# The experts' down projection with the tokens as the stationary side, in a fused attention and mixture-of-experts block

## The reference

```python
def _experts(x_flat, Wg, Wu, Wd):
    g = jax.nn.silu(jnp.einsum('nc,eci->nei', x_flat, Wg))
    u = jnp.einsum('nc,eci->nei', x_flat, Wu)
    return jnp.einsum('nei,eic->nec', g * u, Wd)

def _moe(x, Wgate, expert_bias, Wg, Wu, Wd, sWg, sWu, sWd):
    shared = jnp.mean(_experts(xf, sWg, sWu, sWd), axis=1)
    ...
    routed = jnp.einsum('ne,nec->nc', comb, _experts(xf, Wg, Wu, Wd))
    return (shared + routed).reshape(b, t, c)

xn = _layernorm(x, axis=-1)
x = x + _L0_attn_ref(xn, ...) + _L0_ffn_ref(xn, ...)
```

## Time and profile before

| | |
|---|---|
| median of 3 runs | 1395.76 us (1391.84 to 1400.21) |
| the profiled execution, first to last instruction | 1398.2 us |
| mean granted TensorE clock | 0.960 of full |
| busy share | PE 94%, PEld 66%, DVE 78%, ACT 60%, POOL 51% |
| HBM traffic over the span | 107 GB/s |

### The profile page before, as it was taken

One profiled execution on the slowest core, in us unless ns is written; L12 is line 12 of the kernel. 1 busy time (PEld: TensorE's weight loads), 2 busy tenths in 40 slices (PEclk: granted clock), 3 DMA queues, 4 the chain that ended last, 5 costly groups with the idle time before them and its releaser, 6 DMA issues.

```text
span 1398.2 us, 40108 instructions
## 1 busy us (share of the span) xinstructions
PE 1309.8 (94%) x16484; PEld 923.2 (66%) x16484; DVE 1085.4 (78%) x2298; ACT 844.3 (60%) x1329; POOL 710.1 (51%) x800
## 2 busy tenths in 40 slices
PE   4589999999999999999999999999999999999996
PEld 3456666666766676676766767676666766666654
DVE  7767687977979787887879788887878888787623
ACT  1046566666666666666666666666666666666662
POOL 4434454565455566545555665545556554545112
PEclk8679899999999999999999999999999999999998
DMA  6655455435455544555555445545544454555000
GB/s 192 109 120 125 113 135 128 119 67 124 110 132 136 124 114 85 119 115 124 136 136 125 107 94 112 127 117 135 135 114 113 81 125 113 136 128 125 13 2 16
DMA packets 139993, 156.43 MB, mean 112 GB/s; under 512 B 32896, under 2 KB 126756, under 8 KB 133668
## 3 DMA queue, kind: packets, MB, share of 16 engines
q1 hardware_dynamic: 139812, 153.87, 46.9%
HBM read 83.10 MB, written 67.11 MB: 107 GB/s over the span
## 4 chain that ended last, share of the span: by engine, by line
PE 77%; DVE 12%; POOL 6%; issue 2%; ACT 1%; SPq 1%; DMA 0%; POOLq 0%; DVEq 0%
PE ps L226 24%; PE psm L226 18%; PE pse L226 13%; PE psv L226 13%; DVE R L771 6%; PE ps L353 3%; POOL x2lo L1382 1%; POOL tc_ L1336 1%; PE ps L344 1%; PE ps L419 1%; DVE pB L726 1%; PE ps L361 1%; PE ps L413 1%; POOL kt_ L1345 1%; DVE rt L854 1%
## 5 line engine op out<-in xcount | busy, mean ns | idle before, releaser
L771 DVE TRANSPOSE_TENSOR_REDUCE R<-psm 128x32 f32<-128x1024 f32 x384 | 478.6, 1246 | 163.4 <-PE psm L226 160.5
L1146 ACT ACTIVATE PT<-pse 128x1024 f32<-128x1024 f32 x384 | 393.8, 1025 | 278.3 <-PE pse L226 278.1
L1328 POOL TENSOR_TENSOR ts_<-ts_,pA 128x512 f32<-128x512 f32 x32 | 37.1, 1158 | 374.3 <-DVE pA L717 374.3
L226 PE MATMUL pse<-qsB,ks 128*128 128x512 f32 (+1 forms) x768 | 215.4, 417 | 2.3 <-ACT pse L1150 2.3
L226 PE MATMUL psm<-qsB,ksm 128*128 128x256 f32 (+1 forms) x640 | 139.6, 333 | 20.6 <-DVE R L771 13.6
L1387 POOL TENSOR_TENSOR hT<-th,cbs 128x512 f32<-128x512 f32 x64 | 82.0, 1282 | 132.3 <-ACT cbs L1200 132.2
L1150 ACT ACTIVATE pse<-maskb 128x512 f32<-128x512 bf16 x256 | 143.4, 593 | 4.1
L1160 ACT ACTIVATE OT<-psv 128x512 f32<-128x512 f32 x128 | 76.8, 600 | 93.5 <-PE psv L226 91.6
L226 PEld LDWEIGHTS pse<-qsB,ks 128*128 128x128 f32 (+1 forms) x768 | 108.1, 194 | 32.2 <-ACT pse L1150 13.0
L226 PEld LDWEIGHTS psm<-qsB,ksm 128*128 128x128 f32 x640 | 96.3, 195 | 47.9 <-DVE R L771 30.7
L226 PE MATMUL psv<-PT,vA 128*9 128x128 f32 x3072 | 100.5, 279 | 4.7 <-issue 4.7
(11 more groups left out here) (196 smaller groups left out, 2683.0 us busy)
## 6 DMA issues: line engine op xcount, KB each, us to landing
scrB<-pB SPq DMA_DIRECT2D x64, 768.0 KB, 5.0
qsB<-scrB SPq DMA_DIRECT2D x128, 384.0 KB
scrA<-pA SPq DMA_DIRECT2D x128, 96.0 KB, 2.3
qsA<-scrA SPq DMA_DIRECT2D x128, 64.0 KB
ksA<-scrA SPq DMA_DIRECT2D x128, 64.0 KB
xs<-in_x SPq DMA_DIRECT2D x16, 256.0 KB, 2.9
qsA<-scrA SPq DMA_DIRECT2D x128, 32.0 KB
ksA<-scrA SPq DMA_DIRECT2D x128, 32.0 KB
```

The source lines that it names most:

```text
L226: return e.matmul(o, l, r, start=start, stop=stop, skip_group_check=True)
L771: e.tensor_reduce(red, MX[:].rearrange("p i (c q) -> p (i c) q", q=32), AX.X, ALU.max, apply_transpose=True).then_inc(s_mr, 1)
L1146: e.activation(PT[g % 4], EX[:], ACT.Exp, scale=(8.0 ** -0.5, 0.125)[br]).then_inc(s_pt, 1)
L1328: e.tensor_tensor(rA[:], fA[:], pA[:, 0], ALU.subtract).then_inc(s_ra, 1)
```

## The change

- PE's `moe_d` makes, for each of the five slices, four products instead of one: the stationary side is a block of 128 tokens of `hT`, the moving side `wds` of that slice with its 128 columns. The output has the tokens in the partitions, in four column blocks of the same bank, which is the layout that the transposes gave.
- `moe_t` on PE, `moe_d` on ACT and the tile `dT` go. `moe_out` reads the bank `wd` itself; it is the one that frees it.
- On DVE `moe_out` stands at k = 2 ahead of `stats` and `prep_a0` instead of behind them.
- The shared slice is used with all 128 partitions. POOL sets partitions 64 to 127 of slice 4 of `hT` and of `wds` to zero at the start, between `stats2(0)` and `stats(1)`, and PE's first down projection waits for that.
- `store` waits for the release of `wd`, and `moe_sq` on ACT, which writes `th[0]`, waits for POOL's last `moe_h` of the pair before instead of for the release of `mt`.

```diff
-        sq, dT = th[0], th[1]
+        sq = th[0]
...
                 if fs[0] == 4:
                     wd[0] = claim(w, now, 2, "wd", p)
                     w.wait_ge(s_wb, WD)
+                    w.wait_ge(s_pad, 2)
                 bk, s = wd[0]
                 for f in fs:
-                    M = 128 if f < 4 else 64
                     if f < 4:
                         w.wait_ge(s_h, 4 * p + f + 1)
                     else:
                         released(w, "g", 4, p)
-                    t = mm(bk[:], wds[0:M, f, :], hT[0:M, f, :], f == 4, f == 3)
+                    for i in range(4):
+                        t = mm(bk[:, 128 * i:128 * i + 128], hT[:, f, 128 * i:128 * i + 128], wds[:, f, :], f == 4 and i == 0, f == 3)
...
-            def moe_t(p):
-                bk, f = claim(w, now, 0, "mt", p)
-                released(w, "wd", p)
-                for i in range(4):
-                    t = e.transpose(bk[:, 128 * i:128 * i + 128], dT[:, 128 * i:128 * i + 128], ident[:])
-                t.then_inc(f, 1)
...
                     if k == 3:
-                        if even and done:
-                            moe_t(p - 1)
                         if before:
                             tail_out(c - 1)
...
             def moe_out(p):
-                bk, f = arrived(w, "mt", p)
+                bk, f = arrived(w, "wd", p)
...
                     if k == 2:
+                        if even and done:
+                            moe_out(p - 1)
                         if soon3:
                             stats(n2 + 1)
                         if soon:
                             prep_a0(n2)
                         if odd and moe:
                             moe_hg(p, 4)
-                        if even and done:
-                            moe_out(p - 1)
...
             def moe_sq(p, a):
                 w.wait_ge(s_y, 2 * p + 2)
-                if p >= 1:
-                    released(w, "mt", p - 1)
+                w.wait_ge(s_h, 4 * p)
...
-            def moe_d(p):
-                bk, f = arrived(w, "wd", p)
-                e.activation(dT[:], bk[:], ACT.Copy).then_inc(f, 1)
...
                     if k == 2:
-                        if even and done:
-                            moe_d(p - 1)
                         if odd and moe:
                             moe_c(p)
...
             stats2(0)
+            w.wait_ge(s_pw2, 1)
+            e.memset(hT[64:128, 4, :], 0.0).then_inc(s_pad, 1)
+            w.wait_ge(s_pad, 1)
+            e.memset(wds[64:128, 4, :], 0.0).then_inc(s_pad, 1)
+            w.wait_ge(s_pad, 2)
             stats(1)
...
             def store(p):
-                released(w, "mt", p)
+                released(w, "wd", p)
```

More of the change, by code:

```diff
@@ L169, in build @@
             sem(n) for n in ("s_half", "s_k1", "s_ksi", "s_wa", "s_wn", "s_wb", "s_sa", "s_sb"))
-        s_bv = sem("s_bv")
+        s_bv, s_pad = sem("s_bv"), sem("s_pad")
         s_v, s_g = sem("s_v"), sem("s_g")
```

## The result

| | before | changed |
|---|---|---|
| median, same chip | 1397.65 us (1391.84 to 1400.21, 4 runs) | 1415.43 us (1406.87 to 1419.13, 4 runs) |
| changed / before | | 1.0115, 95% interval 1.0066 to 1.0165 |
| span of the profiled execution | 1398.2 us | 1405.1 us |

The changed kernel is slower by 1.15% (by the two medians alone it would be 1.27%). Ratios, here and in the table of the experiments, are worked out from the faster group of executions alone, while medians and ranges take in all of them, so the two need not agree. The forecast was 1406.5 us and its range ended at 1413: the sign was right, the size was too small. The profiled execution of the changed kernel is the fastest of its four runs, so its span understates the loss.

What follows compares the result with a forecast made beforehand. The prediction took PE to bound the kernel (77% of the chain). Thirteen pairs (+12.3), two pairs without `prep_qk` (-0.4) and the end (-1.2) gave +10.7 us on the median 1395.8: 1406.5 us, range 1397 to 1413.

Steps and rivals of the forecast that it cites:

- products, a pair: PE's down projection: 40 passes of 128 columns instead of 10 of 512 cost +0.18 us a pair.
- change from 64 to 128 rows, padding: PE's down projection: padding costs no columns and the row change merely moves to the step's start; costed at zero.
- transposes, a pair: On PE in even blocks, removing the four transposes of the product is worth -0.40 us a pair.
- wait of `prep_qk` for DVE, a pair: PE's `prep_qk` waits for its bank until DVE's `moe_out`, behind the k = 2 reduction, frees it: +1.17 us.
- together, 13 pairs: Products, wait and transposes summed where `prep_qk` follows the down projection: +0.95 us each, +12.3 in all.
- the pairs without `prep_qk`: At c = 30 and 32 the bank goes to `tail_out`, without a wait: -0.22 us each, -0.4 in all.
- start, memsets: Two POOL memsets between `stats2(0)` and `stats(1)`: cost 0, at worst 0.2 us, or 2.3 once without cover.
- end: After the last product DVE starts 0.04 us later, without ACT and transposes between: -1.2 us once.
- A: Rival: the stall at `prep_qk` is covered, so the kernel is not slower, 1391.3 us; chance 0.15.
- B: Rival: stall covered and earlier `moe_out` shortens the k = 3 reduction's turn on DVE, 1382 us; chance 0.03.
- C: Rival: PE's weight loads show, a pass every 0.192 us instead of 0.112, 1458 us; chance 0.03.
- I put the change on the median: Baseline step: +10.7 us added to the median of the runs, 1395.8, instead of the profiled span, 1398.2.

Runs made afterwards that it cites:

- e4: Changed kernel, but ACT copies the down projection's bank to `dT` at k = 2 and frees it, `moe_out` adds from `dT`; 1395.63 us, ratio 0.9976.
- e5: e4 with the old products of 512 columns and transposes left out, so its output is not the reference's; 1391.44 us, ratio 0.9979.
- e7: Changed kernel with 64 rows again for the shared slice instead of the padded 128; 1408.04 us, ratio 1.0079.
- e6: Kernel before, but DVE instead of ACT copies the bank to `dT`, behind the k = 2 reduction; 1413.42 us, ratio 1.0122.
- e1: The changed kernel, unaltered, timed again beside the kernel before; 1412.9 us over 11 runs, ratio 1.0078.
- e12: The same kernel as e11, run again for a readable trace; 1409.64 us, ratio 1.0119.
- e2: Changed kernel with `moe_out` on DVE ahead of the k = 2 reduction instead of behind it; 1395.09 us, ratio 0.9977.
- e10: Kernel before with the first shared gate product moved from ahead of the k = 9 scores to behind them; 1391.44 us, ratio 0.9945.
- e11: Changed kernel with the first shared gate product moved behind the k = 9 scores; 1414.5 us, ratio 1.0088.
- e9: e2 with the first shared gate product moved from ahead of the k = 9 scores to behind them; 1386.45 us, ratio 0.9917.
- e3: Changed kernel with `moe_out` on DVE behind `stats` instead of ahead of it; 1461.07 us, ratio 1.0434.
- e8: Changed kernel with an unneeded DVE memset of 485 ns ahead of `moe_out`; 1437.46 us, ratio 1.0303.

## Why the prediction missed

**The terms were right.** Against the steps of the forecast, in its order:

| step of the forecast | forecast | measured | where |
|---|---|---|---|
| products, a pair | +0.18 | +0.17 | e4 less e5; 16 passes on the chain 1.79 us, four before 1.72 |
| change from 64 to 128 rows, padding | 0 | 0.01 at most | e7 |
| transposes, a pair | -0.40 | -0.38 | e5 |
| wait of `prep_qk` for DVE, a pair | +1.17 | +1.14 to 1.17 | changed, e6 |
| together, 13 pairs | +0.95 each | +0.93 to 0.96 in 12 (once 1.02), 0.72 or 0.73 in one | changed, e1, e12 |
| the pairs without `prep_qk` | -0.22 each | -0.21 to -0.22 at c = 30; c = 32 has no reductions to compare | changed, e1, e12 |
| start, memsets | 0 | 0: 200 ns the smaller; DVE's next step at 10.10, before 10.11 | changed |
| end | DVE 0.04 behind the product | 1401.61 against 1396.94 + 4.63 = 1401.57 | changed |

The wait was foreseen with its engine, its line and its number. Only its look was off: I expected 1.1 to 1.4 us of idle each in the view, and it shows 0.9 at the matmul and 1.1 at the weight load, since the idle is counted from the end of the last matmul's record, and before, `prep_qk` began while that record still ran (1.14 less 0.89, so 0.25 us).

**The rivals.** A (covered) falls: e2 and e4 show what a kernel without the wait does, -0.21, and the changed one has +0.93. B falls with it. C (weight loads show) falls: 16 passes of 128 columns, each with its load of 192 ns, take 1.79 us, 0.112 each. This bears also on the rule of the Trainium skill that was weighed ("TensorE: Matmul & The Clock Gate", Back-to-back issue gap), by which four short matmuls would cost 2.5 times one long one: here it is 1.79 / 1.72 = 1.04, measured on the very edit; that page's ratio doesn't hold for these fp32 products.

**What failed** is the last step, "I put the change on the median", and the range, which left out the scatter of the executions. The mechanism and its terms were right; the number they were added to and the width around it were not. The miss is 1415.4 - 1406.5 = 8.9 us. With all executions that there are, of the kernel before 93 (mean 1398.2, standard deviation 6.4, 1381 to 1415) and of the changed kernel 15 (mean 1412.3, 7.8, 1397 to 1427), it divides into three parts:
- 2.4 us: the median of three, 1395.8, was low. The three runs that were shown lie within 8.4 us, while executions of this kernel spread over 34. The profiled execution had a span of 1398.2. That this equals the mean of the 93 is chance: a span lies some 2 us below the execution's own time (1405.1 for 1406.87 in the changed kernel). So the span was no better ground than the median; only more executions would have been.
- 3.4 us: the effect is 1412.3 - 1398.2 = 14.1 us by these runs, not 10.7. With the two spreads the standard error is 2.1, so 10.7 isn't excluded, nor is 17. Whether anything beyond the 10.7 is real stays open (below).
- 3.1 us: the four runs of the first result lie above the mean of all 15. That is chance.

Of the width, the bounds of the unknown costs (5.5 us either way) were too wide, since every term came out within 0.03 us a pair; and the scatter of a median of four executions (6 to 8 over 2, 3 to 4 us) with that of the baseline was hardly in it. In hindsight, from the mean of all runs, 1398.2, and with the scatter given its weight, the forecast would have been 1409 and the range 1401 to 1417. The better baseline alone would have moved the upper end to 1415.4, just where the measured 1415.43 lies.

**What the scatter is.** In every kernel the time follows the mean granted clock, by about -1.5 us for +0.001 (slope within kernels over 208 executions, r = -0.84; what is left scatters by 3.4 us). One fall of 3.4 us at half clock lowers the mean of a 1400 us execution by 3.4 x 0.5 / 1400 = 0.0012 and costs 1.5 us by the traces, which is -1.2 us for +0.001: near the slope of the runs, a fifth less. So the falls account for most of the scatter, as a correlation and not as an experiment. Two profiles of the changed program show it side by side (e1 below, the first one above): the same 13 steps, 5.7 us apart, and 5 falls at the routing in e1 against 8.

```profile
core 0: 1399.4 us, clock 0.962
```

This is also why one trace against one trace is a poor measure of the total: changed less before is 6.9 us by spans, while 12.1 come from the 13 pairs alone.

**What stays open** is whether the stall of 0.89 us costs more than its length through the clock. Against it: in five traces with such gaps (changed, e1, e6, e7, e12) no fall stands behind any of 65. For it: the changed kernel with the late gate product runs at a clock 0.006 below that of e10, which accounts for 9 of their 20 us, and the mean of the changed kernel's 15 runs is 0.958 against 0.959 of before, 0.957 against 0.961 for e6 in its own company; but e1 (0.959 against 0.959) and e7 (0.960 against 0.961) show hardly any. Taken at equal clock, changed less before is 12 us, e12 and e11 less e10 is 11: the length of the stalls. The extra 2 to 9 us would have to come from more falls at the routing, where e12 has them in several neighbouring pairs. Counted there, the six traces without the stall (before, e2, e4, e5, e9, e10) have 5 to 9 falls in 16 pairs, 6.7 on the mean, the five with it 5 to 10, 7.8 on the mean, and e3 and e8 with their longer gaps 11 each. That points the same way, and 1.1 falls more at 1.5 us each would be 2 us; but one trace of each kernel can't tell it from chance.

## What to carry to other kernels

When an eviction is removed because a later instruction can read the bank itself, that instruction inherits the bank's release. Look up who claims the bank next, and what stands ahead of the new releaser on its in-order engine; here one DVE reduction of 1.25 us between them cost 1.14 us in each of 13 pairs, and moving the same instruction ahead of the reduction (e2) gave it all back. Size the range of a forecast by the scatter of the executions and take several of them for the baseline: with terms good to 0.03 us a pair, the low median of three and a range without the scatter decided that the forecast missed.

## What the runs showed of the hardware

- **A gap can cost two to three times its length, and not in proportion.** At the same place of the program, gaps of PE of 0.89 us were accompanied by a fall to half clock in 0 of 65 cases, gaps of 1.41 us in 5 of 13 (e8), gaps of 1.97 us in 11 of 13 (e3). Each fall costs 1.5 us or 3.0 us more. The Trainium skill describes such a case ("TensorE: Matmul & The Clock Gate", A second HAM failure mode: psum-queue depth-cycling): in a bf16 kernel, frequent short idling between groups of matmuls while PSUM banks go round was enough to send the clock back and forth. The traces of e3 and e8 agree that short idling is enough, and in them it isn't even frequent: one such gap in some 80 us.
- **Length alone doesn't decide.** At the routing the clock falls behind a gap of 0.79 us, with products of 8 columns ahead of it, in 5 to 11 of 16 pairs, and in e9, e10 and e12 in 6, 7 and 9 pairs with no such gap at all.
- **A small DVE instruction can last as long as a large one of POOL beside it.** In all traces together, 68 times one of the small routing instructions on DVE, 128 x 32, lasts over 2 us instead of about 0.2. Each of these 68 starts within 0.35 us of the start of POOL's 128 x 1024 addition to `pB` and ends 0.04 to 0.05 us behind its end. In the changed kernel:

```profile
431.01 2.45 DVE L846 TENSOR_TENSOR rt<-rt,rs 128x32 f32<-128x32 f32 x1
431.03 2.37 POOL L1326 TENSOR_TENSOR pB<-tc_,pB 128x1024 fp32r<-128x1024 f32 x1
433.49 0.19 DVE L848 TENSOR_TENSOR rt<-rt 128x32 f32<-128x32 f32 x1
```

  In e1's trace, without a fall in this pair, L846 takes 0.19 us. In the kernels with the early gate product this goes with nearly every fall at the routing. In e9, e10 and e12 none lasts over 2 us, and there a fall costs as much (15.55 - 14.07 = 1.48 us), so it isn't what a fall costs. No run moved one of the two instructions alone.
